# Moving the start-up work of a fused state-space, attention and expert kernel: first weight split and input split earlier, input weight's low part and second norm later

## The reference, cut to what matters

```python
xn = layernorm(x)                                  # x: 8 blocks of 512 rows x 256
u  = conv4(xn @ W_in + b_in) + conv_b              # 512 channels
h_t = tanh(A) h_{t-1} + u_t * Bp;  y_t = Cp . h_t + Dp * u_t      # scan over the rows
mamba = silu(y) @ W_out + b_out
attn  = softmax(q k^T / 4) v                       # 16 heads of 16, per block
gate  = softmax(xn @ W_gate + b_gate); the two largest of 8 are kept
moe   = sum_e gate_e * (xn @ W_e + b_e)
out   = x + mamba + attn + moe
```

## Time and profile before

| | us |
|---|---|
| three runs, median (lowest to highest) | 788.93 (787.6 to 789.32) |
| the profiled execution, whole | 787.89 |
| its span, first to last instruction | 786.1 |
| TensorE busy | 753.9 |
| VectorE busy | 581.4 |
| ScalarE busy | 535.4 |
| GpSimd busy | 387.4 |

### The profile page before, as it was taken

How to read it: one execution, slowest core, us unless ns; L and a number is a source line. 1 busy time by engine, 2 the same in 40 slices (tenths; PEclk the granted TensorE clock), 3 DMA queues, 4 the chain that set the end, 5 groups by cost and what they waited for, 6 DMA issues and landing times.

```text
span 786.1 us, 13228 instructions
## 1 busy us (share of the span) xinstructions
PE 753.9 (96%) x4404; PEld 453.3 (58%) x4404; DVE 581.4 (74%) x846; ACT 535.4 (68%) x926; POOL 387.4 (49%) x522
## 2 busy tenths in 40 slices
PE   9689999999998999999999999989999999999996
PEld 7457556565555655556555665556655565555553
DVE  6689876976679875887759876698667987568920
ACT  4637766777666767667567775667666776767775
POOL 8445554455444834456346463445444473435654
PEclk9989999999999999999999999999999999999999
DMA  8301201122110221102111121113111121112000
GB/s 272 69 4 44 68 19 28 38 59 78 35 38 13 79 58 41 42 22 82 35 42 42 45 82 31 38 25 95 42 42 43 32 58 39 46 41 69 23 2 27
DMA packets 32465, 39.09 MB, mean 50 GB/s; under 512 B 8513, under 2 KB 18535, under 8 KB 32398
## 3 DMA queue, kind: packets, MB, share of 16 engines
q1 hardware_dynamic: 31418, 37.29, 18.1%
q10 hardware_dynamic: 980, 0.96, 0.6%
HBM read 8.74 MB, written 4.19 MB: 16 GB/s over the span
## 4 chain that ended last, share of the span: by engine, by line
PE 80%; DVE 13%; issue 4%; ACT 3%; ACTq 0%; DVEq 0%
PE PS L464 39%; PE PS L624 12%; PE SB L591 12%; PE TB L608 7%; PE PS L521 5%; DVE mx L1051 4%; PE PS L480 2%; DVE ys L901 2%; DVE xn L1027 1%; PE PS L631 1%; DVE xl L933 1%; DVE qkl L927 1%; DVE ys L897 1%; PE PS L476 1%; DVE th L1086 1%
## 5 line engine op out<-in xcount | busy, mean ns | idle before, releaser
L1051 DVE TENSOR_REDUCE mx<-SB 128x2 f32<-128x1024 f32 x256 | 312.9, 1222 | 141.0 <-PE SB L591 139.9
L1118 POOL TENSOR_TENSOR acc<-acc,mt 128x256 f32<-128x256 f32 x320 | 247.9, 782 | 251.0 <-ACT mt L675 178.9
L830 ACT ACTIVATE Pt<-TB 128x1024 f32<-128x1024 f32 x251 | 257.7, 1027 | 59.3 <-PE TB L608 56.3
L675 ACT ACTIVATE mt<-PS,cpad 128x256 f32<-128x256 f32 x256 | 107.5, 471 | 58.9 <-PE PS L464 58.5
L591 PE MATMUL SB<-kst,qst 48*128 48x512 f32 x512 | 127.9, 496 | 14.6 <-DVE mx L1051 14.3
L624 PE MATMUL PS<-Pt,V 128*17 128x512 f32 x1024 | 122.3, 595 | 0.0
L591 PEld LDWEIGHTS SB<-kst,qst 48*128 48x128 f32 x512 | 47.7, 183 | 125.3 <-DVE mx L1051 75.1
L464 PE MATMUL PS<-weh,xTh 128*128 128x512 f32 x256 | 109.9, 429 | 2.2 <-DVE xTl L914 1.3
L608 PE MATMUL TB<-qst,kst 50*128 50x512 f32 x502 | 101.2, 398 | 1.1 <-ACT Pt L830 1.0
L464 PE MATMUL PS<-wel,xTh 128*128 128x512 f32 x256 | 100.9, 394 | 0.0
L464 PE MATMUL PS<-weh,xTl 128*128 128x512 f32 x256 | 100.6, 393 | 0.0
(11 more groups left out here) (162 smaller groups left out, 1142.6 us busy)
## 6 DMA issues: line engine op xcount, KB each, us to landing
qst<-qkh SPq DMA_DIRECT2D x124, 64.0 KB, 2.3
kst<-qkh SPq DMA_DIRECT2D x124, 64.0 KB, 2.3
out<-acc SPq DMA_DIRECT2D x8, 512.0 KB, 2.8
qst<-qkl SPq DMA_DIRECT2D x62, 64.0 KB, 2.2
kst<-qkl SPq DMA_DIRECT2D x62, 64.0 KB, 2.3
acc<-in_x SPq DMA_DIRECT2D x7, 512.0 KB, 3.9
Bt<-in_wexp SPq DMA_DIRECT2D x2, 512.0 KB, 7.6
raw<-in_wexp SPq DMA_DIRECT2D x2, 512.0 KB, 8.8
```

The source lines that it names most:

```text
L675: return e.activation(mt[:, item % NM, :], P, ACT.Copy, scale=scale)
L830: e.activation(Pt[:, T % NP, :, :], turned_bank(T)[:, :, :], ACT.Exp, scale=0.25).then_inc(s_ex, 1)
L1051: e.tensor_reduce(mx[:, g % 2, 0:2, 4 * jj + a], SB[:, :, :], AX.X, ALU.max).then_inc(s_mx, 1)
L1118: e.tensor_tensor(v, v, mt[:, item % NM, :], ALU.add).then_inc(s_mt, 1)
```

## The change

The weight split `W_Q0` on ScalarE goes ahead of the first copies, and `krylov(1)` and all later ones move back by one unit (`krylov(7)` to V0, `krylov(8)` to V1, the response to V2). ScalarE makes the input's hi parts in round -1, behind units D0 and D2; GpSimd makes all four low parts before its loop. ScalarE's hi parts of R and E0 move to round 1 and that of E1 to round 2, with R ahead of E0; GpSimd's low parts of E0 and E1 move to rounds 2 and 3; VectorE's Rl moves to round 3, bst and sst to round 4, and the input weight's low part to round 5, behind maximum 5. Q0.2 may be dealt from round 5 on, the B units from 6 on, and the second block's norm starts in round 7 (LN[1] = 7). Empty rounds on TensorE get six idle turns instead of four, in rounds 0 to 3 instead of 0 to 7.

By the new values the planner gives: round 5 Z0.1, Q0.2; 6 B0 to B3, with banks 0, 1, 2, 0; 7 Q0.3, Y0.0; 8 X0.0, M0.0, M0.1; and other places for units in rounds 9 to 100. B2's bank is the one that Q0.2 had.

```diff
-    at, xh, ln = {}, {0: -1}, {0: -1, 1: 5}
+    at, xh, ln = {}, {0: -1}, {0: -1, 1: 7}
...
-            return max(after(("T", b, 1), 1), 32 * b - 10 if i < 2 else 32 * b + 6 if b else 7)
+            return max(after(("T", b, 1), 1), 32 * b - 10 if i < 2 else 32 * b + 6 if b else 5 if i == 2 else 7)
         if kind == "B":
-            return 5
+            return 6
...
-KRYLOV = {("T", 1): (2, 3), ("D", 0): (4,), ("D", 1): (5,), ("D", 2): (6,), ("D", 3): (7,)}
+KRYLOV = {("T", 1): (1, 2), ("D", 0): (3,), ("D", 1): (4,), ("D", 2): (5,), ("D", 3): (6,)}
...
-            for s in range(2):
-                krylov(s)
-                idle_turns(2)
+            krylov(0)
+            idle_turns(2)
...
-                    if t == 0 and (u.kind, u.i) == ("V", 0):
-                        krylov(8)
-                    if t == 0 and (u.kind, u.i) == ("V", 1):
+                    if t == 0 and u.kind == "V" and u.i < 2:
+                        krylov(7 + u.i)
+                    if t == 0 and (u.kind, u.i) == ("V", 2):
...
-                if 0 <= t < 8 and not AT[t]:
-                    idle_turns(4)
+                if 0 <= t < 4 and not AT[t]:
+                    idle_turns(6)
...
-                if t == 0:
-                    split(W_E0)
-                elif t == 1:
+                if t == 1:
                     e.wait_ge(s_bw, 2)
                     e.copy(bst, bwr).then_inc(s_wh, 1)
-                    split(W_E1)
-                elif t == 2:
                     e.wait_ge(s_rr[0], 64)
                     e.wait_ge(s_rr[1], 64)
                     e.copy(Rh[:, :], Rraw).then_inc(s_Rh, 1)
+                    split(W_E0)
+                elif t == 2:
+                    split(W_E1)
...
-            for s in range(2):
-                krylov(s)
             split(W_Q0)
+            krylov(0)
...
-                        if (u.kind, u.i) == ("T", 1):
-                            split(W_VG)
-                            split(W_QK)
...
+                            if u.kind == "T":
+                                split((W_VG, W_QK)[s - 1])
+                        if u.kind == "D" and u.i % 2 == 0:
+                            x_hi(0, u.i)
+                            x_hi(0, u.i + 1)
...
-                for b in range(NB):
+                for b in range(1, NB):
                     if 0 <= t - XH[b] < 4:
                         x_hi(b, t - XH[b])
...
-                if t == 2:
+                if t == 3:
                     e.wait_ge(s_Rh, 1)
                     e.tensor_tensor(Rl[:, :], Rraw, F(Rh[:, :]), ALU.subtract).then_inc(s_Rl, 1)
-                elif t == 3:
-                    split(W_IN)
+                elif t == 4:
...
+                if t == 5:
+                    split(W_IN)
...
+            def x_lo(b, a):
+                e.wait_ge(s_xh, 4 * b + a + 1)
+                e.tensor_tensor(xln[:, a, :], xn[:, a, :], F(xhn[:, a, :]), ALU.subtract).then_inc(s_xl, 1)
...
+            for a in range(4):
+                x_lo(0, a)
...
-                if t == 1:
+                if t == 2:
                     split(W_E0)
-                elif t == 2:
+                elif t == 3:
                     split(W_E1)
```

More of the change, by code:

```diff
@@ L1210, in _ @@
             e.tensor_tensor(bwr, bwr, cbr, ALU.add).then_inc(s_bw, 1)
+            for a in range(4):
+                x_lo(0, a)
             for t in range(-1, END + 1):
[L1212 to L1216, removed]
+                for b in range(1, NB):
+                    if 0 <= t - XH[b] - 1 < 4:
+                        x_lo(b, t - XH[b] - 1)
                 for u in early(t) + late(t):
```

## The result

The changed kernel takes 790.58 us (median of 17 runs, 788.89 to 793.17) where the one before takes 789.05 (17 runs, 787.6 to 789.47): ratio 1.0022, interval 1.0014 to 1.003. It is slower by 0.2%, and its times spread more than twice as wide. The profiled execution took 789.92 with a span of 788.1. I had forecast a gain of 2.4 us; the change costs about 1.7.

What follows compares the result with a forecast made beforehand. TensorE was taken to bound the kernel, busy 753.9 of 786.1 us; 2.75 + 0.9 - 1.0 - 0.25 = 2.4 us gain gave 786.3 us, own range 785.4 to 787.3, wider range 784.0 to 788.6.

Steps and rivals of the forecast that it cites:

- What bounds; the wait at Z0.0: Start: Z0.0 waited 2.97 us for GpSimd's input low parts; freed, it starts behind R's low part at 36.3, 3.2 sooner.
- 0.15 of lead: Start: the first weight split ahead of the second squaring lets row transfers leave 0.15 us sooner, bounds 0 and 1.2.
- VectorE's chain: Rounds 3 to 6: GpSimd's splits hold up VectorE; Q0.2's low part ends at 48.2, B2 waits; score 8 lead 2.75.
- The clock: Score 7 and Q0.3 run at 1.2 GHz after the wait for B2: 1.0 us lost, bounds 0 and 1.7.
- the sum: Rounds up to score 8: followed unit by unit, score 8 starts at 52.35 before the clock's price, against 55.10 before.
- After score 8: TensorE's wait of 0.9 us for Q0.3's low part falls away; lead 3.65, or gain 2.65 after the clock.
- Second norm two rounds later: Re-planned rounds 10 to 98: waits for maxima change by 0 plus or minus 1.5 us, 0.25 taken as lost.
- The sign that I had set for this step: Forecast wrong if waits for maxima from 60 to 330 us differ from 3.7 by more than 2.
- Rival 4: Rounds 7 to 11: VectorE carries maxima, convolution, statistics and xn, scores wait; loss 2.9 us, 791.6; chance 0.10.
- Rival 1: Rounds 5 to 8: no clock drop, or one that waits absorb; gain 3.4 us, 785.3; chance 0.20.
- rival 2: Start: VectorE's chain runs unblocked by GpSimd's splits and no clock drop; gain 5.0 us, 783.7; chance 0.07.
- Rival 3: Start: gain returned, E2 ahead of the step rows' low part or R late by itself; 788; chance 0.25.

Runs made afterwards that it cites:

- experiment 6: Changed kernel with VectorE's low part of the output weight at the end of round 15 instead of 13: 789.57 us, ratio 1.0001.
- experiment 9: Changed start with the old plan, but the input weight's low part in round 4, ahead of the bias and step rows: 788.51 us, ratio 0.9994.
- experiment 5: Changed kernel with Q0.2's low part on VectorE ahead of maximum 6 instead of behind it: 789.43 us, ratio 1.0011.
- experiment 8: Changed kernel with 16 idle turns on TensorE between B1 and B2 of round 6: 790.8 us, ratio 1.0027.
- Experiment 12: Changed start with the old plan and more idle turns, 12 instead of 6 in round 3 and 8 between B0 and B1: 785.45 us, ratio 0.9959.
- experiment 7: Changed kernel with Q0.2's low part ahead of maximum 6 and the output weight's low part in round 15: 786.39 us, ratio 0.9971.
- experiment 1: Changed kernel with the planner's three numbers set back, so the changed start with the old plan: 785.58 us, ratio 0.9963.
- experiment 2: Kernel before with only LN[1] = 7 instead of 5, the second block's norm two rounds later: 796.02 us, ratio 1.0099.
- experiment 3: Changed kernel with only LN[1] set back to 5: 791.23 us, ratio 1.004.
- experiment 4: Changed start with the old plan, but Q0.2 in round 5, B0 to B3 and Y0.0 in 6, Q0.3 in 7: 788.65 us, ratio 0.9995.
- experiment 10: Kernel before with only the input's hi parts in round -1 and its four low parts on GpSimd ahead of the loop: 787.18 us, ratio 0.9977.
- experiment 11: Changed start with the old plan, but the squaring and first weight split in their old order: 787.15 us, ratio 0.9976.

## Why the prediction was wrong

*What bounds; the wait at Z0.0.* Right. GpSimd's four low parts run from 19.11 to 21.92, and Z0.0 starts behind R's low part, at 36.81 for 36.3. The half microsecond is the response: after V2 it comes at 23.47 instead of 23.00, where I had taken it 0.15 sooner, and the rows land later (R's hi part at 31.48, waiting 1.10 for its transfer). The term "0.15 of lead" had the wrong sign.

*VectorE's chain.* Right in mechanism and size. q0 took 1.22, the input weight's low part 1.81 (I had put 2.2), Q0.2's low part was done at 47.90 for 48.2, B2 started at 47.96. Experiments 6 and 9 show the blocking with the same operations in two places (1.42 against 3.58, 0.68 against 2.77). The Trainium skill's rule ("SBUF — State Buffer", "Who interferes with whom") held for all of them: q0 ended with GpSimd's E1 (39.15 and 39.10), the input weight's low part 1.07 us after E2.

*The clock.* Under-sized. I took 1.0 with a bound of 1.7; the wait was followed by a low stretch of 6.8 us. Between scores 7 and 8 alone it cost 2.0 (experiment 5), and from B2 to score 8 it is 6.54 us where the forecast had 4.15 and experiment 8, at the full clock, 4.06: the term was 2.4 to 2.5, not 1.0, and above its bound. Score 8 came at 54.50, where the sum gave 52.35 + 1.0 = 53.35. The Trainium skill's account ("TensorE: Matmul & The Clock Gate", "HAM oscillation — how this bites in real kernels"), that each such wait is paid for at the low clock behind it, was nearer than my 1.0. It does not hold for every wait of that size here: the one of 2.06 us for maximum 14 had none behind it.

*After score 8.* The wait for Q0.3's low part fell away, as forecast; the lead at maximum 9 is 1.9, for 2.65.

*"Second norm two rounds later", the re-plan.* This is the step that failed: "0 plus or minus 1.5, and I take 0.25 lost". From maximum 9 to 104 the changed kernel lost 4.0 us: 2.5 of them are idle time of TensorE, 1.5 the low stretch at 155.9. Experiment 12, with the old plan, went through the same units with a lead of 2.70 at maximum 9 and of 2.69 at 104. I priced the re-plan by the waits that the old plan had, as if a new plan could only make these longer or shorter. But it puts other work of fixed rounds, which the planner does not move, in new company. In round 13 the output weight's low part, which had taken 2.72 in the old plan, came behind a first convolution step and silu's product, with GpSimd adding through nearly all of the round (71.87 to 77.53), and took 3.58 in front of a maximum. Repairing this hole gives about 1.7 us, with B2's 4.0 (experiments 6, 7).

As large a loss stands far from the start, and nothing that I ran touches it. From maximum 81 to 104 the lead falls by 2.1 us in the changed kernel, and by 2.1 to 2.2 in each of experiments 5 to 8, which have its plan. In experiments 1 to 4 and 9 to 12, which have the old plan in these rounds, it moves by 0.1 or less. So these 2.1 us are the plan's, shown by the traces. Which order in them would repair it is not tested. A smaller hole stands where T2.0 and T2.1 share round 40: 1.3 us for xn, and the clock low at 155.9 to 159.4. That one was not tested either.

The sign that I had set for this step could not have caught it. Waits for maxima from 60 to 330 us are 4.3 in all in one view, against 3.7, well within my 2. The loss came also as waits for xn (1.9 against 0.7), as low clock, and as a wait behind 330 us.

*The rivals.* Rival 4 had the sign and VectorE behind the maxima as its mechanism, but in rounds 7 to 11 and by the norm; it happened in round 13, by a split. As to the norm itself, experiments 2 and 3 disagree (7 to 8 us worse on the old kernel, no worse in the changed one), and its price by itself stays open. Rival 1 is out, as the clock did fall, and rival 2, as VectorE was held up. Rival 3 has part of its condition: R was late by itself (its hi part at 31.48, where I had 30.8), but E2 did not get ahead of the step rows' low part, which took 0.68. The range was too narrow because the re-plan's bound of 1.5 came from no row of a new plan.

## What to carry to other kernels

When an edit feeds a planner, price it in two parts: the engines' orders with the old plan, and the plan by itself, looking in the new plan for every piece of work that is tied to a round number (here a weight's low part) and for what it now stands beside. Look through all rounds that the plan changes, not only those near the edit: compare the two traces at points where the same units are done, and see between which of them the lead goes. On an engine whose result gates TensorE each round, put work with two SBUF inputs where GpSimd is idle, and ask of each bank what its release stands behind. Price a new TensorE wait twice, with a low stretch behind it and without: here the waits of 2.28, 3.10 and 3.35 us had one, that of 2.06 had none in one profile.

## What the runs showed of the hardware that was not expected

One and the same kernel takes different times, and the stretches at 1.2 GHz are a large part of it: 12 runs of experiment 6 lie between 786.86 and 791.16 us, in two groups that go with mean clocks of 0.991 to 0.993 and 0.985 to 0.987. In the changed kernel the three slowest runs (791.95 to 793.17 us) have 0.987, and the seven fastest (788.89 to 789.92) 0.991. The mean clock is not all of it, since two runs at 0.991 took 790.58 and 791.64. The two kernels with the highest clocks, experiments 1 and 12 (0.993 to 0.999, five runs each), are the fastest and spread by only 1.1 and 0.8 us.

A four-partition VectorE subtraction that takes 0.68 us elsewhere took 2.77 us where it began inside a GpSimd split of 2.89 us, and ended 0.56 us behind it (experiment 9).
